# Graph attention and expert layers on one core: narrower destination one-hots, and sixteen of the v2 sums moved to later heads

## The reference

```python
h = (x @ W).reshape(N, H, C)                       # layer 1: H = 4 heads of C = 512; layer 2: one head of 768
al_s = einsum('nhc,hc->nh', h, a_src)              # one number per node and head
al_d = einsum('nhc,hc->nh', h, a_dst)
e = leaky_relu(al_s[src] + al_d[dst], 0.2)
m = segment_max(e, dst); ex = exp(e - m[dst])
alpha = ex / (segment_sum(ex, dst)[dst] + 1e-16)
out = segment_sum(h[src] * alpha, dst) + bias      # layer 1 is followed by elu
```

## Time and profile before

| What | Value |
|---|---|
| median of the runs | 1366.8 us |
| the profiled execution's own time | 1367.77 us |
| its span, first to last instruction | 1366.0 us |
| TensorE / VectorE / ScalarE busy | 1239.5 / 895.7 / 610.3 us |
| mean granted TensorE clock | 0.959 of full speed |

### The profile page before, as it was taken

How to read it: one execution, slowest core, us unless ns; L and a number is a source line. 1 busy time by engine, 2 the same in 40 slices (tenths; PEclk the granted TensorE clock), 3 DMA queues, 4 the chain that set the end, 5 groups by cost and what they waited for, 6 DMA issues and landing times.

```text
span 1366.0 us, 18379 instructions
## 1 busy us (share of the span) xinstructions
PE 1239.5 (91%) x7111; PEld 811.3 (59%) x7111; DVE 895.7 (66%) x1766; ACT 610.3 (45%) x1108; POOL 162.3 (12%) x144
## 2 busy tenths in 40 slices
PE   4997776987997999799989999999998889999996
PEld 3664443444544554455578888888654756666664
DVE  7989889989878987898724662444677333333440
ACT  5668434657435743596610662011321234444441
POOL 1000000000000000000000000400011834344322
PEclk9999997998998999999999999999799999999999
DMA  8243260343134312400655212512300487667532
GB/s 201 104 130 122 81 201 22 94 131 117 57 90 133 118 58 74 125 24 2 226 164 163 69 53 53 175 35 80 105 1 10 128 253 178 176 169 181 163 63 31
DMA packets 69922, 148.87 MB, mean 109 GB/s; under 512 B 10597, under 2 KB 34661, under 8 KB 69210
## 3 DMA queue, kind: packets, MB, share of 16 engines
q1 hardware_dynamic: 63179, 130.44, 31.3%
q0 software_dynamic: 6656, 17.26, 6.4%
HBM read 115.09 MB, written 34.59 MB: 110 GB/s over the span
## 4 chain that ended last, share of the span: by engine, by line
PE 51%; DVE 27%; ACT 8%; issue 7%; DMA 4%; POOL 2%; SPq 0%; POOLq 0%; DVEq 0%; ACTq 0%
PE PS L1727 44%; DVE sb L1359 4%; DVE sb L1380 3%; DVE sb L1278 3%; DVE sb L1395 2%; DVE sb L1388 2%; PE PS L1864 2%; DVE sb L1440 2%; DVE sb L1429 2%; DVE sb L1331 2%; DVE sb L1249 1%; PE PS L1769 1%; DVE sb L1447 1%; ACT sb L991 1%; ACT sb L981 1%
## 5 line engine op out<-in xcount | busy, mean ns | idle before, releaser
L1727 PE MATMUL PS<-sb,sb 128*125 128x384 f16 (+8 forms) x4404 | 784.6, 338 | 42.3 <-DVE sb L1254 23.7
L1727 PEld LDWEIGHTS PS<-sb,sb 128*125 128x125 f16 (+3 forms) x4404 | 541.8, 129 | 269.9 <-issue 59.8
L1864 PE MATMUL PS<-sb,sb 125*128 125x375 f16 (+1 forms) x1440 | 267.2, 347 | 0.0
L1864 PEld LDWEIGHTS PS<-sb,sb 125*128 125x128 f16 x1440 | 141.9, 99 | 122.0 <-issue 13.7
L981 ACT ACTIVATE sb<-sb 125x375 f32<-125x375 f32 (+1 forms) x150 | 81.5, 544 | 133.9 <-DVE sb L1380 133.5
L1571 DVE SCALAR_TENSOR_TENSOR sb<-sb,sb 128x2304 f16<-128x2304 f32 x27 | 68.8, 2558 | 89.4 <-ACT sb L1102 89.4
L795 POOL TENSOR_TENSOR sb<-sb,sb 125x768 f32<-125x768 f32 x10 | 18.0, 1841 | 845.5 <-DMA sb<-in_x_dram 845.5
L1380 DVE SCALAR_TENSOR_TENSOR sb<-sb,sb,sb 125x375 f32<-125x375 f32 (+1 forms) x150 | 95.4, 637 | 8.7 <-ACT sb L975 8.7
L975 ACT ACTIVATE sb<-sb,sb 125x375 f32<-125x375 f32 (+1 forms) x150 | 93.7, 628 | 4.8 <-DMA sb<-aa_d 4.8
L1395 DVE TENSOR_TENSOR sb<-sb,sb 125x375 f16<-125x375 f32 (+1 forms) x150 | 87.9, 586 | 0.1
L1388 DVE SCALAR_TENSOR_TENSOR sb<-sb,sb 125x375 f32<-125x375 f32 (+1 forms) x150 | 87.7, 585 | 0.1
(11 more groups left out here) (190 smaller groups left out, 1091.3 us busy)
## 6 DMA issues: line engine op xcount, KB each, us to landing
sb<-in_L_ffn_w_dram SPq DMA_DIRECT2D x24, 1152.0 KB, 5.6
sb<-in_L_gnn_W_dram SPq DMA_DIRECT2D x32, 384.0 KB, 4.2
sb<-xt_d SPq DMA_DIRECT2D x30, 375.0 KB, 4.4
sb<-mask_d SPq DMA_DIRECT2D x20, 546.9 KB
sb<-h_d SPq DMA_DIRECT2D x10, 1000.0 KB, 5.5
h_d<-sb SPq DMA_DIRECT2D x16, 375.0 KB, 4.0
sb<-aa_d SPq DMA_DIRECT2D x5, 1093.8 KB
h_d<-sb SPq DMA_DIRECT2D x8, 500.0 KB, 4.5
```

The source lines that it names most:

```text
L1727: ins = M(out_, lhs(a), rhs(b), start=first and a + b == 0, stop=last and a == 1)
L1864: ins = M(PS[:, t, 0:n], hb[:, i, pa, 128 * c:128 * c + 128], P[:, i, pb, lo:lo + n], start=i == 0 and pa + pb == 0, stop=i == NT - 1 and ...
```

## The change

It has two parts. First, an edge tile's destination one-hot covers the tile's own range of destinations (`span`, 23 to 38 of them, so 230 to 380 columns) in place of one or two whole chunks. The columns of a chunk are now ordered destination first, source tile second (`p (n i)`), so that a range is one run; the key is 10 times the destination plus the source tile. TensorE multiplies, for each chunk met, only the columns of the range that lie in it, and the copies out of PSUM reorder. OR has 16 slots in place of 8. Second, of the 32 v2 sums 10 stay in the counts, 6 in head 1's projection, and 8 each are made in heads 1 and 2 (two in each of groups 6, 8, 10 and 12) with their own row tile WVL, vector tile A2L and new loads on SP; `v2_split` runs three times.

```diff
-    RO, RG, PG = 8, 2, 2
+    RO, RG, PG = 16, 2, 2
-    met = [[c for c in range(NC) if -EC - MARGIN < c * EC - t * T < T + MARGIN] for t in range(ET)]
+    span = [[d for d in range(N) if -EN - MARGIN < d * EN - t * T < T + MARGIN] for t in range(ET)]
+    span = [(d[0], d[-1] + 1) for d in span]
+    met = [range(a // DC, (b - 1) // DC + 1) for a, b in span]
...
-        V2_H1 = [4, 2, 2, 2, 2, 2, 2, 2, 2, 2]
+        V2_H1 = [1, 1, 1, 1, 1, 1, 0, 0, 0, 0]
+        V2_AT = {6: 0, 8: 1, 10: 2, 12: 3}
...
+            def load_a2(h):
+                sp.wait_ge(s_mu, NT * (h + 2))
+                sp.dma_start(A2L[:, 0, :], as2.to_broadcast([128, D])).then_inc(s_a2v, 16)
+                sp.dma_start(A2L[:, 1, :], ad2.to_broadcast([128, D])).then_inc(s_a2v, 16)
+
+            def load_v2_row(ch):
+                sp.wait_ge(s_va, 2 * ch)
+                sp.dma_start(WVL[:, :], W2[128 * ch:128 * ch + 128, :]).then_inc(s_wv[1], 16)
...
-                A(CT[:, :, c * DC:c * DC + DC], PS[0:T, c % 3, 0:KC].rearrange("p (i n) -> p i n", n=DC), ACT.Copy
+                A(CT[:, :, c * DC:c * DC + DC], PS[0:T, c % 3, 0:KC].rearrange("p (n i) -> p i n", n=DC), ACT.Copy
...
-            link(V.tensor_scalar(EQ[:, 1, :], EF[:, 1, :], 1.0 / DC, 0.5 / DC - 0.5, ALU.mult, ALU.add))
...
-                    c, w = met[t][0], len(met[t])
-                    V.tensor_scalar(OR[:, t % RO, 0:w, :], iok[:, 0:w, :], float(SP * c), KEY[:, t:t + 1], ALU.add,
+                    a, w = NT * span[t][0], NT * (span[t][1] - span[t][0])
+                    V.tensor_scalar(OR[:, t % RO, 0:w], iok[:, 0:w], float(a), KEY[:, t:t + 1], ALU.add,
...
-                        v2_split()
+                        v2_split(0, V2_FIRST)
+                    if h and h + 1 < H and g in V2_AT:
+                        v2_sums(2)
+                    if h and h + 1 < H and g == NG - 1:
+                        v2_split(CH * (h + 1), CH * (h + 2))
...
-                        ins = M(place, OL[:, t, :], OR[:, t % RO, w, :], start=False, stop=t == reach[c][1] - 1)
+                        ins = M(place[:, NT * (lo - c * DC):NT * (hi - c * DC)], OL[:, t, :],
+                                OR[:, t % RO, NT * (lo - first):NT * (hi - first)],
+                                start=False, stop=t == reach[c][1] - 1)
```

More of the change, by code:

```diff
@@ L69, in build @@
     NC = N // DC
-    EC = NE // NC
+    EN = NE // N
     MARGIN = 250
     KC = NT * DC
-    SP = 512
-    assert ET % 2 == 0 and KC <= SP and EC * NC == NE
-    met = [[c for c in range(NC) if -EC - MARGIN < c * EC - t * T < T + MARGIN] for t in range(ET)]
+    assert ET % 2 == 0 and KC <= 512 and EN * N == NE
+    span = [[d for d in range(N) if -EN - MARGIN < d * EN - t * T < T + MARGIN] for t in range(ET)]
+    span = [(d[0], d[-1] + 1) for d in span]
+    met = [range(a // DC, (b - 1) // DC + 1) for a, b in span]
     reach = [(min(t for t in range(ET) if c in met[t]), max(t for t in range(ET) if c in met[t]) + 1)
              for c in range(NC)]
-    assert all(1 <= len(m) <= 2 for m in met)
+    assert all(1 <= len(m) <= 2 and b - a <= DC for m, (a, b) in zip(met, span))
     assert all(reach[c][0] >= reach[c - 3][1] for c in range(3, NC))
@@ L117, in build @@
     MSK = MSKL[0]
-    W2G = [at(o + 3072 * b, [128, D], F32) for b in range(3)]; o += 10048
+    W2G = [at(o + 3072 * b, [128, D], F32) for b in range(3)]
+    A2L = at(o, [128, 2, D], F32)
+    WVL = at(o + 6144, [128, D], F32); o += 10048
     o += 32
@@ L131, in build @@
     o_a = o
-    ROWM = at(o, [T, N], F32); o += 5024
+    ROWM = at(o, [T, N], F32)
+    VJL = at(o, [128, D], F32); o += 5024
     assert o <= 207008, o
@@ L475, in build @@
         V2_B = [1] * NT
-        V2_H1 = [4, 2, 2, 2, 2, 2, 2, 2, 2, 2]
+        V2_H1 = [1, 1, 1, 1, 1, 1, 0, 0, 0, 0]
+        V2_AT = {6: 0, 8: 1, 10: 2, 12: 3}
+        V2_FIRST = 2 * CH
+        V2_USES = len(range(4, V2_FIRST, 5))
         W2_STEPS = [0, 0, 0, 0, 0, 0, 1, 1, 1, 2, 2, 2, 2, 2, 2]
@@ L651, in _ @@
                         load_w1_rows(h + 2, range(2, 4))
+                    if h:
+                        load_v2_row(CH * (h + 1) + 1)
                     chain_shift(h + 1)
+                    if h:
+                        load_v2_row(CH * (h + 1) + 2)
                     if h + 2 < H:
                         load_w1_rows(h + 2, range(4, KD))
+                    if h:
+                        load_v2_row(CH * (h + 1) + 3)
+                    if h + 2 < H:
+                        for i in range(3):
+                            load_xt(h + 2, i)
+                    else:
+                        sp.dma_start(WRG[:, :, :], Wr.rearrange("(k p) e -> p k e", p=128)).then_inc(s_wrl, 16)
+                    store_h1(NB * h + 1)
+                    if h:
+                        sp.wait_ge(s_va, 2 * CH * (h + 2))
                     if h + 2 < H:
@@ L1759, in counts @@
                         pe.wait_ge(s_or, min(t + PG, ET))
-                    for w, c in enumerate(met[t]):
+                    for c in met[t]:
                         place = PS[0:T, c % 3, 0:KC]
+                        lo, hi = max(span[t][0], c * DC), min(span[t][1], (c + 1) * DC)
+                        first = span[t][0]
                         if t == reach[c][0]:
@@ L1874, in al2 @@
                 pe.wait_ge(s_y6, CH * (k + 1))
-                if k == 0:
-                    pe.wait_ge(s_vs, 1)
+                if b == 0 and h != 1:
+                    pe.wait_ge(s_vs, max(h, 1))
                 for c in range(CH):
```

75 lines of the change are left out of this document (37 added, 38 removed).

## The result

The changed kernel took 1358.6 us (median of nine runs, 1354.4 to 1363.3) against 1366.8 us for the kernel before (nine runs, 1363.8 to 1368.6). The ratio is 0.994, 95% interval 0.9925 to 0.996: 8.2 us faster, where 14.4 were forecast. Its profiled execution took 1358.96 us, span 1357.2, mean clock 0.954.

What follows compares the result with a forecast made beforehand. TensorE and VectorE were both nearly full in the counts' first part, VectorE the bound in the second. Terms -0.8 - 8 - 10 - 11 + 15.4 = -14.4 us gave 1352 us, range 1343 to 1364.

Steps and rivals of the forecast that it cites:

- One-hots, 0.23 us each: VectorE in the counts: a one-hot of 370 or 380 columns costs 0.23 us, bounds 0.20 and 0.26.
- The rival that they don't get cheaper below 500 columns: One-hots stay at 0.26 us each, VectorE gains only 0.10 us each: 1356 us, chance 0.09.
- Products, 0.10 us on average: TensorE in the counts: 286 products of 222 columns on average take 0.10 us each, saving 31 us of TensorE time.
- I take no change: PSUM copies and chunk starts striding over 40 bytes cost nothing more; other end, 15 copies twice as long, 8 us on ScalarE.
- where 8 stood: First part of the counts: 8 us saved by narrower one-hots and products, bounds 5 and 10.5.
- Counts, second part, 10 us: From 98 to 161 us, where VectorE is the bound: cheaper one-hots save 10 us, bounds 6 and 13.
- my second rival: Counts get another bound, TensorE's falling clock or ScalarE: they bring 9 in place of 18 us, 1361 us; chance 0.22.
- my three signs of being wrong: Stretches from group 5's denominator grow under 4 us; VectorE waits for in_L_gnn_W or ScalarE in counts; second-part clock not 1.00.
- Head 1's projection, 11 us: Removing v2 sums of 0.97 us from the chain there, and loads from SP's list, saves 11 us; bounds 8 and 12.
- Heads 1 and 2, 7.2 + 8.2 us: Eight added sums per head and small splits lengthen these heads, together 15.4 us; bounds 7 and 18.
- the late rows: Rival: new W2 row loads come late in heads 1 and 2 and VectorE waits: 1374 us, chance 0.09.
- the hidden sums: Rival: moved sums mostly fit VectorE's idle time in heads 1 and 2, costing 8 not 15.4 us: 1345 us, chance 0.20.

Runs made afterwards that it cites:

- e9: Changed kernel with each chunk cleared in order by a zero-weight product, unit columns added by small products, out-of-range path left out: 1358.6 us, ratio 0.992.
- e11: As e10, plus idle TensorE products in the second part of the counts: 1349.7 us, ratio 0.986 to the kernel before.
- e4: Changed kernel with the pairs of sums in groups 9, 10, 12, 14 and row loads behind the broadcast: 1356.2 us, ratio 0.9915 to the kernel before.
- e10: Kernel before with the change's one-hots alone and the ordered chunk starts of e9, sums not moved: 1354.7 us, ratio 0.989.
- e2: Kernel before with only the moved sums, their loads and splits, one-hots still wide: 1371.1 us, ratio 1.0026.
- e1: Kernel before with only the change's one-hots, chunk starts and copies, sums and loads as before: 1352.1 us, ratio 0.987.
- e7: As e1, plus idle TensorE products in the second part of the counts: 1351.0 us, ratio 0.988 to the kernel before.
- e8: As e7, with two v2 sums taken from head 1's first tile into VectorE's wait for the row from memory: 1355.1 us, ratio 0.991 to the kernel before.
- e3: Changed kernel with chunk starts reading SBUF at a stride and writing PSUM in order: 1359.9 us, ratio 0.9946 to the kernel before.
- e6: Changed kernel plus idle 500-column TensorE products in the second part of the counts: 1358.6 us, ratio 0.9937 to the kernel before.
- e5: The changed kernel run again, unchanged: 1358.1 us, ratio 0.9926 to the kernel before.

## Why the prediction was right in sign and too high in size

The time lies in the range and on the right side; 6.2 us of the 14.4 are missing. Point by point:

- **One-hots, 0.23 us each: right.** 2.28 us for ten, and the single ones of 230 and 300 columns took 0.19 and 0.21 us, on the forecast's line of 0.13 us fixed and 0.13 for each 500 columns. The rival that they don't get cheaper below 500 columns is out.
- **Products, 0.10 us on average: right**, 0.10 to 0.11. The weight rule of the Trainium skill ("TensorE: Matmul & The Clock Gate", LDWEIGHTS; 104 ns for 125 columns) would give an average of 0.12, by estimate. The trace does not agree: twelve products in 1.22 us are 0.102 each, wide ones included, and the transposes of 125 columns, one every 0.059 us, stay below its figure. So the row was the better guide.
- **"I take no change" for the chunk starts: failed.** The other end that I gave was for the copies only. ScalarE's copies read PSUM at a stride for the same 0.581 us as before; it is TensorE's strided write that doubled, 0.42 against 0.21 us. e9 to e11 price it at 1.5 us of the first part. With it the first part saved 5.7 us, where 8 stood; without it 7.1. The rest of the gap is in my sum: the 10 and 46 that I counted as products include six starts, which keep their 500 columns, and with the 50 others at 0.11 us the first part comes to 7.5 us. A tile with 14 products and a start I put at 5.9 us, where my own prices give 6.1 (0.64 + 3.89 + 1.4 + 0.21); the trace has 6.34, and 6.18 with ordered starts. The 0.8 us at the start are not shown: head 0's first low half came at 34.6 us before and at 34.2 to 35.9 in the eleven kernels with narrow one-hots, 34.2 in the changed one.
- **Counts, second part, 10 us: right up to the last one-hot, and lost in part behind it, where the clock did not hold.** From the last low half to the last one-hot the kernels with narrow one-hots took 51.8 to 53.5 us against 62.6 before, whether the clock fell there or not. The changed kernel's profile took 53.3, and then 3.7 us more than before up to head 1's first low half (13.7 for 10.0), in the half-speed transposes and the projection (6.25 us for 3.89). e4, e9 and e10, whose clock fell as well but not behind the last one-hot, need 9.5 us there and save 10.8 to 10.9 in the whole part. This was my second rival's mechanism, and of my three signs of being wrong two came true: a clock below 1.00 and waits for ScalarE (these are a weak sign, as the kernel before had 2.9 us of them). Its 1361 us is nearer to the result than my 1352, though the counts lost less than it says: they brought 11.3 us in this profile for its 9, and 14.2 by the means of the kernels (57.4 and 64.0 us). The step that failed is that the sum takes the stage at a clock of 1.00 while my own estimate leaves TensorE idle for 22 of 51 us there, and does not ask where in the stage TensorE is the chain. By the stages the price is 2.5 us on average and 5.5 in the changed kernel's profile, 4.2 of them behind the last one-hot; the medians don't show it.
- **Head 1's projection, 11 us: right to a bit low.** 12.8 in the profile, 11.3 in e2, and 11.7 by the means with and without the sums (70.7 over e1, e7, e8, e10, e11; 59.1 over the changed kernel, e3 to e6, e9). In single profiles it was 8.8 to 13.0, and the spread is in one place, the tile behind xt_d's load: 6.4 to 8.2 us from low half to low half, but 10.3 and 10.5 in e9 and e5, where that load took longest (8.7 us) and the clock was at 1.2 GHz for 6.8 us from about its end. So the 1.8 us above the forecast in the changed kernel's profile are as likely luck. The other tiles have the forecast periods, 7.3 us with one sum (from 185.02 to 192.29 in the chain) and 6.4 without (to 198.69), and TensorE waits for xt_d's load at tile 3 as before.
- **Heads 1 and 2, 7.2 + 8.2 us: right, the best term.** 7.4 and 8.2 us in the profile, and nearly the same in the six other kernels that have the sums there. The broadcast is issued 3.3 us later in head 1 (23.1 us behind the denominator of group 5 against 19.8) and 4.1 in head 2 (19.5 against 15.4), for 3.3 and 3.9 forecast. There was no wait for a row of W2 beyond 0.3 us, so neither the late rows nor the hidden sums. The reason that I gave, that the wait for the broadcast "moves behind" the sums, is only half of it: e4 put a pair into the wait and issued the broadcast at the old place, and the period stayed. VectorE's work is the bound on both sides.

The sum of the stages in the profiles is consistent: 0.4 + 5.7 + 5.6 + 12.8 - 0.6 - 7.4 - 8.2 + 0.5 = 8.8 us, the difference of the spans. As for the medians, the one-hots alone brought 11.9 to 18.7 us in five kernels, 15.3 on average, for the forecast's 18.8; and with the sums moved as well the gain was 8.2 to 12.0 in six, 9.3 on average. So moving the sums cost about 6 us in their company and 2.9 alone, where my terms make it +4.4 (15.4 less 11); the spans of the profiles give 4.0 and 3.2. About 3.5 of the missing 6.2 us are thus the one-hots' (strided starts, the sum of the first part, and clock). The other 2.7 are not assigned: the sums' terms hold by the stages, and a difference of that size lies within what such medians differ by.

The rest of the span behind head 3 has the same code in all thirteen kernels and took 702.3 and 701.8 us in the two profiles of the changed kernel, 702.8 before, and 704.7 to 706.6 in the five with the one-hots alone. It goes with the clock: with 44 to 46 us at 1.2 GHz there it took 700.8 to 702.3, with 51 to 53 it took 702.8 to 705.0, and with 54 to 58 it took 704.7 to 706.6. What stays open is why the clock is low longer in some executions than in others, and whether the kernels with the one-hots alone tend to it. Low stretches that move like this can also be why the changed kernel's runs spread over 9 us; either way differences of 2 us were not settled by four to six runs each.

## What to carry to other kernels

Work moved from one stage where VectorE is the bound to another is paid again in full, and here with interest, since in the first place part of it had been covered by a load; each part of a change is worth pricing alone, because one of them may be a loss. When a layout is turned so that the large operand is read in order, look at what now strides, and on which engine: here the copies cost nothing more, the matmul's output stride about twice its time and its input stride four times. And where TensorE gets much less to do, write its clock into the forecast itself and not into a rival, at the place where the chain runs over TensorE: elsewhere in the stage the low clock cost next to nothing.

## What the runs showed of the hardware

- A product of 500 columns took 0.21 us with both sides in order, 0.38 us from start to start (0.42 by the chain) writing PSUM at a stride of 40 bytes, and 0.82 us reading SBUF at a stride of 2500 bytes (all at 2.4 GHz). The read and the write were not tried with each other's stride, so which part is the side's and which the stride's stays open. ScalarE's copy of the same 500 columns out of PSUM, read at the same 40 bytes, took 0.581 us before and after.
- One-hots of 230, 300, 370 and 380 columns took 0.19, 0.21, 0.23 and 0.23 us from start to start, those of 500 and 1000 before 0.26 and 0.39: 0.13 us and 0.26 ns for each column, down to 230.
- Products of 20 to 60 columns, each with its own load of 125 weight columns, took down to 0.03 us from start to start in the changed kernel, transposes of 125 columns 0.059 us before.
- The idle products kept the granted clock at 1.00 in every fifth of 92 to 152 us in e6, e7 and e8, and in all but the first (0.86) in e11, and did not lengthen the stage (61.2 to 62.5 us). Without them it fell in all seven profiles with the narrow one-hots, down to 0.57 in a fifth of the changed kernel's and to 0.77 in e10's, and what that cost differed: 61.7 to 67.0 us for the stage. With the wide one-hots it was 1.00 in the kernel before and fell to 0.86 in e2.
- The same low clock cost next to nothing where VectorE was the bound (13.7 us of it in e9, 52.3 us for a stretch of 51.8 to 52.2 without), and 4.2 us where the chain ran over TensorE (9.8 us of it in the changed kernel, 13.7 for 9.5 us).
